# Second round of the feed-forward set into the first, two batches' sums to one PSUM bank, and changed ends of the attention in a block of feed-forward, attention and feed-forward

## The chip, the cores and the metric

One Trainium2 chip, one core of it. The metric is the device time of one execution in microseconds (us). TensorE is called PE here, VectorE DVE, ScalarE ACT, GpSimd POOL, and SyncE SP; SP only issues DMAs. A DMA that POOL issues has its descriptors written by POOL itself.

## What is computed

The input x is 8 batches of 2048 tokens of 256 floats. A token-routed feed-forward is applied with half weight, then an attention, then the same feed-forward again. All arithmetic is fp32 (the attention's scores and values run through fp32r tiles in part).

```python
x = x + 0.5 * ffn(layernorm(x))        # ffn returns its input, with 128 rows a batch replaced
x = x + attn(layernorm(x))
x = x + 0.5 * ffn(layernorm(x))

def ffn(x):                            # x: (8, 2048, 256)
    _, idx = top_k(x @ w_router, 128)              # 128 tokens of each batch, in order of score
    x_sel = take(x, idx)
    h = rmsnorm(x_sel, g1)
    q, k, v = split(h @ W_qkv.T)                   # 16 heads of 16
    att = softmax(causal(q @ k.T / 4))             # 128 x 128 a head
    x_attn = (att @ v) @ W_out.T
    h2 = rmsnorm(x_sel + x_attn, g2)
    x_ff = silu(h2 @ W1.T) * (h2 @ W2.T) @ W3.T    # 682 wide
    return x.at[idx].set(x_sel + x_attn + x_ff)

def attn(x):                           # 8 heads of 32, all 2048 tokens of a batch
    q, k, v = (lowrank(x, U, V) + b for each)
    return softmax(q @ k.T / sqrt(32)) @ v
```

## The kernel before

The program is a row of blocks; between two of them all engines meet at a barrier and the block's semaphores are cleared. `score_rows` reads all rows, takes their statistics and router scores. `pick_tokens` finds the 128 best of each batch and keeps their row numbers in `picked`. `routed_ffn` gathers those rows, computes the feed-forward on them and scatters them back. `project` makes keys, queries and values of all tokens. `attend` is the attention. Then `score_rows`, `pick_tokens` and `routed_ffn` once more, now on the sum of `after_ffn` and `attention`. Each engine has its own list of instructions, written by hand in the order in which it takes them, and waits on semaphores. An engine that waits holds up all that stands behind in its list.

**Reading.** In the second `score_rows` SP loads pieces of 4 tiles (128 rows each) of both addends, 512 KB each. The addend goes into a ring of `NADD = 6` buffers; a load waits until the sum of six pieces earlier is done (`added`). POOL adds each piece (L198) and makes one product (L191).

**Picking.** Each batch is cut in four lists. DVE finds the 128 best of every list, then for each batch b counts for each candidate how many are better (L474), turns the rank into a 0/1 table `is_rank` (L484), and PE multiplies this table by the row numbers (L516), which gives the rows in order in `prow`. After the last batch one DVE copy (L489) turns all of `prow` into `picked`, and the block ends. ACT scales all other rows beside this and stores them.

**Feed-forward.** Two rounds (`ROUNDS`) of `NB = 4` batches. POOL first issues all gathers: 8 in the first feed-forward (L649), 16 in the second (L649 and L652), then makes constants, and in the second adds the two gathered parts (L672). One round is, in this order on PE: turn the normalised rows (L910), keys and queries (L917), values (L926), for each batch the scores of all 16 heads into banks 0 to 3 (L937), for each batch turn the probabilities and multiply by the values (L949, L961), output projection (L967), turn the second norm's rows (L973), six `up` steps (L984, two projections of 128 columns each) and six `down` steps (L993) that sum into banks 0 to 3, a bank for each batch. DVE spreads the keys by head (L757), adds the causal mask (L764), takes the row maximum (L768), normalises six of sixteen heads (L775; POOL does ten, L681), combines the values' halves (L789), and gates (L810, L812). ACT does the exponentials, 16 a batch (L869), copies out of PSUM and the tanh of the gate (L896). Round 1 begins when round 0's `down` has been issued.

**Attention.** 64 units (batch, four heads, 512 queries). A unit's scores come in 64 tiles; ACT takes the exponential (L1703). Before that the row maximum is found one unit ahead: PE writes 4 score tiles into `ps_max` (L1736), DVE reduces three of them (L1592), ACT copies the fourth (L1655) and DVE reduces the copy (L1594); 16 such fours a unit. For unit 0 this stands alone at the start, with one set of four banks: PE writes the next four only when both readers are done. Its loads are `load_q(0, 0)` and `load_kv(0, 0)` on SP, all of them landed before PE starts. The sum of a unit's probabilities is made by POOL (L1562) on nine of sixteen chunks and by accumulating DMAs that POOL issues (L1541, seven pairs of chunks, `DMA_PAIRS`); PE sums over partitions (`close_z`, L1792), then two sets of turns and a DVE multiplication end the unit.

## Time and profile before

| | us |
|---|---|
| median of 3 runs | 4295.17 (4293.64 to 4295.38) |
| profiled execution | 4294.03 |
| its span, first to last instruction | 4292.0 |
| 0 to 171 | first reading and picking |
| 171 to 434 | first feed-forward |
| 434 to 721 | projections |
| 721 to 796 | attention: loads, row maxima of unit 0 |
| 796 to 3791 | attention: 64 units |
| 3791 to 3816 | attention: end of the last unit |
| 3816 to 4012 | second reading and picking |
| 4012 to 4292 | second feed-forward |

Over the span PE is busy 84%, DVE 74%, ACT 76%, POOL 70%. The rows of the section further down are of this one execution; times in them count from the span's start.

### The profile page before, as it was taken

To read this page: it belongs to the slowest core of one execution; us is meant where nothing else is said; L and a number is where in the kernel's file an instruction comes from. 1 tells how busy PE (TensorE), PEld (TensorE's weight loads), DVE (VectorE), ACT (ScalarE), POOL (GpSimd) and SP (SyncE) were. 2 spreads that over 40 slices of the span, in tenths; PEclk is the share of its full clock that TensorE was granted. 3 is DMA by queue.
4 is the path that set the end of the run, shared out by engine and by line. 5 is a ranking of instruction groups with operands and counts; after the bars stand their busy time and mean duration, and the time that the engine had idled before them with its cause. 6 is when DMAs were issued, how large, how long until landed. Compare 5 with 4: busy or idle time off the path is not lost. (4 is left out here: it accounts for less than half of the span.)

```text
span 4292.0 us, 59690 instructions
## 1 busy us (share of the span) xinstructions
PE 3592.8 (84%) x20178; PEld 1422.3 (33%) x20178; DVE 3187.8 (74%) x4122; ACT 3242.9 (76%) x6717; POOL 2988.4 (70%) x1166
## 2 busy tenths in 40 slices
PE   0376784699999999999999999999999999930376
PEld 0243452233333333333333333333333333310243
DVE  8644674888888888888888888888888888628544
ACT  3544673589988898998898899899889989834433
POOL 2011001399999999999999999999999989975211
PEclk9988897799999999999999999999999999965598
DMA  6500899589999999999999999999999999888300
GB/s 210 168 5 3 296 391 313 118 180 194 210 198 204 206 199 205 198 212 198 204 207 197 207 196 209 202 202 208 198 207 200 206 202 195 170 214 277 124 5 5
DMA packets 335683, 809.46 MB, mean 189 GB/s; under 512 B 27596, under 2 KB 211424, under 8 KB 271648
## 3 DMA queue, kind: packets, MB, share of 16 engines
q0 software_dynamic: 66432, 475.04, 54.9%
q1 hardware_dynamic: 223008, 284.46, 22.7%
q10 hardware_dynamic: 45952, 46.27, 3.1%
q8 instruction: 159, 2.61, 0.2%
q14 instruction: 132, 1.08, 0.1%
HBM read 198.90 MB, written 136.48 MB: 78 GB/s over the span
## 5 line engine op out<-in xcount | busy, mean ns | idle before, releaser
L1703 ACT ACTIVATE at_probs<-at_ps_s 128x512 f32<-128x512 f32 x4096 | 2261.9, 615 | 256.4 <-PE at_ps_s L1813 248.9
L1562 POOL TENSOR_TENSOR at_pool_sum<-at_pool_sum,at_probs 128x2048 f32<-128x2048 f32 x448 | 2173.6, 4852 | 27.8 <-DMA at_probs<-at_probs 20.0
L1592 DVE TENSOR_REDUCE at_part_max<-at_ps_max 128x3 f32<-128x1536 f32 x1024 | 1801.0, 1759 | 428.6 <-PE at_ps_max L1736 428.3
L1813 PE MATMUL at_ps_s<-at_qs,at_ks 97*128 97x512 f32 (+1 forms) x4096 | 1524.4, 451 | 6.4 <-ACT at_probs L1703 5.1
L1782 PE MATMUL at_ps_acc<-at_probs,at_v 128*32 128x512 f32 x8192 | 1092.7, 605 | 0.9 <-ACT at_probs L1703 0.9
L1813 PEld LDWEIGHTS at_ps_s<-at_qs,at_ks 97*128 97x128 f32 (+1 forms) x4096 | 626.5, 188 | 1103.5 <-ACT at_probs L1703 815.5
L1594 DVE TENSOR_REDUCE at_part_max<-at_max_copy 128x1 f32<-128x512 f32 x1024 | 691.7, 675 | 0.0
L1655 ACT COPY at_max_copy<-at_ps_max 128x512 f32<-128x512 f32 x1024 | 610.0, 596 | 102.2 <-PE at_ps_max L1736 102.0
L1541 POOL DMA_DIRECT2D at_probs<-at_probs x448 | 399.7, 892 | 288.4 <-ACT at_probs L1703 240.1
L1736 PE MATMUL at_ps_max<-at_ks,at_qs 32*128 32x512 f32 x4096 | 525.5, 500 | 83.0 <-DMA at_ks<-qk_parts 49.3
L1736 PEld LDWEIGHTS at_ps_max<-at_ks,at_qs 32*128 32x128 f32 x4096 | 197.8, 183 | 442.2 <-issue 393.4
L1562 POOL TENSOR_TENSOR at_pool_sum<-at_probs 128x2048 f32<-128x2048 f32 x64 | 313.0, 4891 | 0.1
L1782 PEld LDWEIGHTS at_ps_acc<-at_probs,at_v 128*32 128x32 f32 x8192 | 161.2, 108 | 346.3 <-ACT at_probs L1703 299.4
L1525 POOL MEMSET at_ones<- 128x128 f32 x1 | 0.2, 204 | 285.9 <-POOLq L62 285.9
L681 POOL TENSOR_TENSOR f_att<-f_att,f_rowsum 128x1280 f32<-128x1280 f32 x16 | 49.5, 3097 | 182.3 <-DVE f_rowsum L773 182.3
L285 PE MATMUL s_pt<-s_ident,s_small 128*128 128x128 f32 x2 | 0.9, 448 | 203.6 <-DVE s_small L254 203.6
L75 ACT ACTIVATE rows_tile<-rows_tile,rows_affine 128x256 f32<-128x256 f32 x256 | 129.3, 587 | 19.1 <-ACT rows_tile L75 13.8
L1607 DVE RECIPROCAL at_rz<-at_ps_s 128x16 f32<-128x16 f32 x64 | 16.5, 257 | 169.6 <-PE at_ps_s L1799 169.6
L1255 PE MATMUL pr_pqk<-pr_xT,pr_w 128*128 128x512 f32 x256 | 124.0, 629 | 16.2 <-ACT pr_xT L1202 12.0
L869 ACT ACTIVATE f_att<-f_att,f_rowmax 128x128 f32<-128x128 f32 x256 | 98.7, 388 | 47.7 <-DVE f_rowmax L769 47.7
L1155 DVE SCALAR_TENSOR_TENSOR pr_lo<-pr_pqk,lr_bias,pr_hi 128x512 fp32r<-128x512 f32 x128 | 88.4, 744 | 40.4 <-ACT pr_hi L1214 37.1
L224 DVE BATCH_NORM_STATS2 s_stats<-rows_tile 128x6 f32<-128x256 f32 x256 | 101.2, 419 | 20.2 <-POOL rows_tile L198 20.2
(196 smaller groups left out, 2405.0 us busy)
## 6 DMA issues: line engine op xcount, KB each, us to landing
at_probs<-at_probs POOLq DMA_DIRECT2D x448, 1024.0 KB, 8.3
qk_parts<-pr_hi SPq DMA_DIRECT2D x32, 1024.0 KB, 12.1
qk_parts<-pr_lo SPq DMA_DIRECT2D x32, 1024.0 KB, 12.3
at_qs<-qk_parts SPq DMA_DIRECT2D x320, 64.0 KB, 5.5
at_ks<-qk_parts SPq DMA_DIRECT2D x80, 256.0 KB, 5.2
rows_tile<-in_x SPq DMA_DIRECT2D x16, 1024.0 KB, 11.9
after_ffn<-rows_tile ACTq DMA_DIRECT2D x16, 1024.0 KB
v_tokens<-pr_v SPq DMA_DIRECT2D x32, 512.0 KB, 10.9
```

The costliest lines, as they stand in the source:

```text
L75: return nc.scalar.activation(self.tile[:, b, t, :], self.tile[:, b, t, :], ACT.Identity, scale=self.affine[:, 0, b, t:t + 1], bias=self.a ...
L224: nc.vector.bn_stats(stats[:, b, t, :], rows.tile[:, b, t, :]).then_inc(stats_done, 1)
L1255: nc.tensor.matmul(pqk[:, m, :], w[:, m // NG, m % NG, :], xT[:, n % 2, m % NG, :], start=True, stop=True).then_inc(qk_done, 1)
L1541: nc.gpsimd.dma_start(probs[:, slot(unit, a)], probs[:, slot(unit, c)], accum_op=ALU.add).then_inc(dma_added[(unit * ND + d) % MERGES_OUT] ...
L1562: nc.gpsimd.tensor_tensor(acc, first, probs[:, slot(unit, c)], ALU.add).then_inc(pool_added, 1)
L1592: nc.vector.reduce_max(part_max[:, 0:HG - 1, t, c], ps_max[:, 0:HG - 1], AX.X).then_inc(three_max_done, 1)
L1594: nc.vector.reduce_max(part_max[:, HG - 1:HG, t, c], max_copy[:, n % 2:n % 2 + 1], AX.X).then_inc(part_max_done, 1)
L1655: nc.scalar.copy(max_copy[:, n % 2], ps_max[:, HG - 1]).then_inc(max_copied, 1)
L1703: nc.scalar.activation(probs[:, slot(unit, c), h], ps_s[:, BANK[unit, j]], ACT.Exp, scale=SCALE).then_inc(exp_done, 1)
L1736: last = nc.tensor.matmul(ps_max[:, h], qs[rows, unit % NQB, h, t * P:(t + 1) * P], ks[rows, un % BU // NU, h, c * 512:(c + 1) * 512], sta ...
L1782: last = nc.tensor.matmul(ps_acc[h * DH:(h + 1) * DH, :], v[:, k // NU, c, h * DH:(h + 1) * DH], probs[:, slot(n, c), h], start=(c == 0), ...
L1813: nc.tensor.matmul(ps_s[:, BANK[unit, j]], ks[rows, g, h, c * P:(c + 1) * P], qs[rows, unit % NQB, h, :], start=True, stop=True).then_inc( ...
```

## The change

Six things are edited.

1. **Feed-forward order.** `qT` and `v` get a buffer for each round. Keys, queries, values of round 1 are issued between the score steps of round 0. A batch's scores are now two half steps of 8 heads in two banks (`bank_scores`), masked one half at a time. Round 1's scores, masks and exponentials are issued between the `up` and `down` steps of round 0. After them comes round 1 from the turned probabilities on, as before. POOL does all eight multiplications, then all eight scatters.
2. **`down` banks.** Two batches' sums share a bank (banks 0 and 1); the last row step waits for both of a bank.
3. **Gathers.** A new class `Gathered` holds `xs`, `ads` and their semaphores; POOL issues batch b's gathers inside `pick_tokens` as soon as `picked` has that batch. `is_rank` has two buffers instead of one for each batch, and the copy into `picked` is made batch by batch.
4. **Buffers.** To make room, `NADD` goes from 6 to 4 and the scrap buffers of `score_rows` from 4 to 2.
5. **Attention start.** Only the high parts of unit 0's queries (SP) and keys (ACT's queue) are loaded first, and PE waits for those alone; SP issues the rest once they have landed. Unit 0's maxima use two sets of four banks in turn (`first_banks`).
6. **Attention end.** The last unit has five POOL additions instead of eight and six accumulating DMAs instead of seven; `close_z_of_last` lets PE sum five sources (two raw chunks, two DMA sums, the POOL sum) instead of one.

```diff
 def pick_tokens
+            for b in range(B):
+                pool.wait_ge(picked_done, b + 1)
+                gathered.gather(b)
...
+                if b >= 1:
+                    copy_picked(b - 1)
-                nc.vector.tensor_tensor(is_rank[:, first:end, :],
+                nc.vector.tensor_tensor(is_rank[:, b % 2],
...
-            dve.wait_ge(ordered, 1)
-            nc.vector.tensor_copy(picked, prow[:]).then_inc(picked_done, 1)
-            dve.wait_ge(picked_done, 1)
+            copy_picked(B - 1)
 def routed_ffn, tensor
+            def scores(i, k):
+                s, g = k // 2, k % 2
+                if k == 0:
+                    pe.wait_ge(qT_copied, i * NC + NC)
+                    pe.wait_ge(v_copied, i + 1)
+                pe.wait_ge(spread_done, at(i, s))
+                if i == 0 and k >= 2:
+                    pe.wait_ge(masked_done, k - 1)
+                elif i > 0:
+                    pe.wait_ge(masked_done, i * HALVES + k)
...
+            up(0, 0)
+            scores(1, 0)
+            up(0, 1)
+            up(0, 2)
+            scores(1, 1)
+            put_down(0, 0)
+            up(0, 3)
+            scores(1, 2)
...
+            scores(1, 7)
+            put_down(0, 5)
+            turn_probs_and_pv(1)
 routed_ffn, vector
+            mask(1, 0)
+            gate(0, 0)
+            mask(1, 1)
+            gate(0, 1)
+            mask(1, 2)
+            gate(0, 2)
+            mask(1, 3)
+            normalize(1, 0)
+            gate(0, 3)
+            mask(1, 4)
+            mask(1, 5)
+            normalize(1, 1)
+            gate(0, 4)
+            mask(1, 6)
+            gate(0, 5)
+            mask(1, 7)
 attend, sync
-            load_q(0, 0)
-            load_kv(0, 0)
+            for to, first, end in HI_ROWS:
+                sp.dma_start(qs[to:to + DH, 0, first:end].bitcast(F32), src[0, 0, :, first:end, 0:UQ]).then_inc(hi_in, 16)
+            sp.wait_ge(hi_in, 2 * len(HI_ROWS) * 16)
...
 attend, tensor
-            pe.wait_ge(q_in[0], LOADS)
-            pe.wait_ge(k_in[0], LOADS)
+            pe.wait_ge(hi_in, 2 * len(HI_ROWS) * 16)
...
+                        sources = [probs[:, slot(n, c)] for c in LAST_RAW]
+                        for d in LAST_PAIRS:
+                            m = n * ND + d
+                            pe.wait_ge(dma_added[m % MERGES_OUT], (m // MERGES_OUT + 1) * 16)
+                            sources.append(probs[:, slot(n, DMA_PAIRS[d][0])])
+                        pe.wait_ge(pool_added, n * ADDS + LAST_ADDS)
+                        sources.append(pool_sum[:, k % 2])
```

PE at the start of a feed-forward, before (L910 turns rows, L917 keys and queries, L926 values, L937 scores, L949 turns probabilities):

```order
L910 MATMUL f_ps<-f_ident,f_hn 128x128 x8
L917 MATMUL f_ps<-f_hT,w_wqkv 128x512 x8
L926 MATMUL f_ps<-w_wqkv,f_hT 128x256 x8
L937 MATMUL f_ps<-f_kspread,f_qT 128x512 x16
L949 MATMUL f_ps<-f_ident,f_att 128x128 x16
```

The same place in the changed kernel (L1007, L1015, L1035, L1050, L1065 are the same five steps):

```order
L1007 MATMUL f_ps<-f_ident,f_hn 128x128 x8
L1015 MATMUL f_ps<-f_hT,w_wqkv 128x512 x8
L1035 MATMUL f_ps<-w_wqkv,f_hT 128x256 x8
L1050 MATMUL f_ps<-f_kspread,f_qT 128x512 x4
L1007 MATMUL f_ps<-f_ident,f_hn 128x128 x8
L1050 MATMUL f_ps<-f_kspread,f_qT 128x512 x4
L1015 MATMUL f_ps<-f_hT,w_wqkv 128x512 x4
L1050 MATMUL f_ps<-f_kspread,f_qT 128x512 x4
L1015 MATMUL f_ps<-f_hT,w_wqkv 128x512 x4
L1050 MATMUL f_ps<-f_kspread,f_qT 128x512 x4
L1035 MATMUL f_ps<-w_wqkv,f_hT 128x256 x8
L1065 MATMUL f_ps<-f_ident,f_att 128x128 x16
```

Round 1's turns, keys, queries and values have moved in front of round 0's turned probabilities.

ACT after the second norm of round 0, in the changed kernel (L953 the last copy of the norm, L961 tanh, L930 exponentials of round 1, L941 the copies of turned probabilities); before, all six tanh (L896) stood in a row there:

```order
L953 ACTIVATE f_hT<-f_ps,w_gain 128x512 x2
L961 ACT_TABLE_LOAD
L961 ACTIVATE f_sig<-f_ps 128x512 x2
L930 ACTIVATE f_att,f_rowsum<-f_att,f_rowmax 128x128 x16
L961 ACTIVATE f_sig<-f_ps 128x512 x2
L930 ACTIVATE f_att,f_rowsum<-f_att,f_rowmax 128x128 x16
L961 ACTIVATE f_sig<-f_ps 128x512
L961 ACTIVATE f_sig<-f_ps 42x512
L930 ACTIVATE f_att,f_rowsum<-f_att,f_rowmax 128x128 x32
L941 COPY f_attT<-f_ps 128x1024 x8
```

The four exponential groups of round 1 now stand among and behind round 0's tanh steps.

POOL around the end of picking, before (L440 the last constant of the picking block, L368 and L644 its end and the next block's start):

```order
L440 CAST t_floats<-t_ints 128x192
L368 UNCONDITIONAL_BRANCH
L61 ISA
L644 UNCONDITIONAL_BRANCH
L649 DMA f_xs<-in_x,picked 128x256 x8
L655 MEMSET f_ones 128x128
```

And now:

```order
L462 CAST t_floats<-t_ints 128x192
L372 DMA g_xs<-in_x,picked 128x256 x8
L390 UNCONDITIONAL_BRANCH
L61 ISA
L678 UNCONDITIONAL_BRANCH
L681 MEMSET f_ones 128x128
```

The gathers have moved from behind the block boundary to ahead of it.

## Rows read from the trace of the kernel before

**Rows 1.** Busy time in stretches: us, each engine's busy us (instructions), PE clock, DMA share, GB/s
```profile
796.00:3746.00 2950.00, 2942.48 (x17173) 1038.59 (x17169) 2430.84 (x2198) 2644.05 (x5227) 2692.60 (x942) 1.00 0.95 199
...
4047.00:4166.00 119.00, 87.48 (x384) 48.66 (x384) 52.49 (x83) 51.89 (x170) 12.39 (x4) 0.86 0.00 1
```

**Rows 2.** Order of time (start, us, instruction, idle before), end of second picking, DVE and PE
```profile
4006.23 0.60 DVE L474 TENSOR_SCALAR_CACHE_REDUCE t_junk<-t_all_top,t_topT 128x384 f32<-128x384 f32 x1
...
4009.89 1.87 PE L516 MATMUL t_prow<-t_rowT,t_is_rank 128*128 128x1 f32 x8 [1.65 <-DVE t_is_rank L484]
...
4011.80 0.17 DVE L489 CAST picked<-t_prow 128x8 uint32<-128x8 f32 x1 [1.96 <-PE t_prow L516]
```

**Rows 3.** The chain that ended last (start, us, what), gathers of the second feed-forward
```profile
4013.73 1.09 POOL f_xs L649
...
4032.68 0.94 POOL f_ads L652
...
4035.13 2.74 POOL f_xs L672 x4
```

**Rows 4.** First feed-forward in order of time: POOL's first gather, DVE's first step behind the constants
```profile
171.45 1.16 POOL L649 DMA_INDIRECT f_xs<-in_x,picked  x1 [80.39 <-POOLq L62]
...
182.91 0.16 DVE L703 TENSOR_REDUCE f_parity<-f_head_of 128x2 f32<-128x8 f32 x1 [10.55 <-POOL f_head_of L666]
```

**Rows 5.** Attention start in order of time: PE's first four, then DVE
```profile
743.47 0.80 PE L1736 MATMUL at_ps_max<-at_ks,at_qs 32*128 32x512 f32 x4 [49.28 <-DMA at_ks<-qk_parts]
...
746.98 1.76 DVE L1592 TENSOR_REDUCE at_part_max<-at_ps_max 128x3 f32<-128x1536 f32 x1 [0.32 <-PE at_ps_max L1736]
```

**Rows 6.** DMA issues from 720 to 800: size each, median us to landing
```profile
at_ks<-qk_parts SPq DMA_DIRECT2D x10, 256.0 KB, 6.8
```

**Rows 7.** Attention end in order of time: PE a unit earlier and at the end, POOL
```profile
3762.22 1.04 PE L1792 MATMUL at_ps_s<-at_pool_sum,at_ones 128*32 128x512 f32 x8
...
3806.85 1.94 PE L1792 MATMUL at_ps_s<-at_pool_sum,at_ones 128*32 128x512 f32 x8 [15.52 <-POOL at_pool_sum L1562]
...
3785.88 1.61 POOL L1541 DMA_DIRECT2D at_probs<-at_probs  x1
...
3792.22 14.48 POOL L1562 TENSOR_TENSOR at_pool_sum<-at_pool_sum,at_probs 128x2048 f32<-128x2048 f32 x3
```

**Rows 8.** DMA issues from 3740 to 3816, and from 3816 to 3936: size, median us to landing
```profile
at_probs<-at_probs POOLq DMA_DIRECT2D x9, 1024.0 KB, 7.6
...
s_addend<-attention SPq DMA_DIRECT2D x32, 512.0 KB, 8.9
```

**Rows 9.** POOL's last two additions of the second reading
```profile
3915.24 2.35 POOL L198 TENSOR_TENSOR rows_tile<-rows_tile,s_addend 128x1024 f32<-128x1024 f32 x1
...
3918.23 2.35 POOL L198 TENSOR_TENSOR rows_tile<-rows_tile,s_addend 128x1024 f32<-128x1024 f32 x1
```

**Rows 10.** The chain that ended last, second feed-forward
```profile
4046.99 1.95 PE f_ps L910 x8
...
4131.72 13.38 PE f_ps L984 x24
...
4146.83 3.43 PE f_ps L984 x8
...
4205.42 12.42 ACT f_att L869 x64
```

**Rows 11.** Groups by line from 4047 to 4284: count, busy us, mean ns of one
```profile
L764 DVE TENSOR_TENSOR f_att<-f_ps,f_causal 128x2048 f32<-128x2048 f32 x8 | 18.3, 2288 | 10.1 <-PE f_ps L937 10.1
L768 DVE TENSOR_REDUCE f_rowmax<-f_att 128x16 f32<-128x2048 f32 x8 | 18.3, 2286 | 0.3
...
L810 DVE SCALAR_TENSOR_TENSOR f_act<-f_sig,f_ps 128x512 f32<-128x512 f32 (+1 forms) x12 | 8.2, 686 | 52.5 <-ACT f_sig L896 52.5
L775 DVE TENSOR_TENSOR f_att<-f_att,f_rowsum 128x768 f32<-128x768 f32 x8 | 7.7, 958 | 0.3
L896 ACT ACTIVATE f_sig<-f_ps 128x512 f32<-128x512 f32 (+1 forms) x12 | 7.2, 596 | 49.7 <-PE f_ps L984 49.7
```

More of the change, by code:

```diff
@@ new lines, in final_row @@
+            def final_row(i, s):
+                dve.wait_ge(down_done, at(i, s | 1))
+                own.step(nc.vector.tensor_tensor(proc[:, s, :], down(s), xr[:, s, :], ALU.add))
+                if i > 0:
+                    dve.wait_ge(row_out, i * NB * 16)
+                nc.vector.scalar_tensor_tensor(row[:, s, :], proc[:, s, :], 0.5, xs[:, at(i, s) - 1, :],
+                                               ALU.mult, ALU.add).then_inc(row_done, 1)
+            for s in range(NB):
+                spread(0, s)
@@ new lines, in _ @@
+            mask(1, 0)
[14 more added lines that the diff above has]
+            mask(1, 7)
+            normalize(1, 2)
+            for s in range(NB):
+                final_row(0, s)
+            normalize(1, 3)
@@ L830, in _ @@
+            for s in range(NB):
+                even_and_odd(1, s)
+            second_norm(1)
+            for f in range(DFF_TILES):
+                gate(1, f)
+            for s in range(NB):
+                final_row(1, s)
         @block.scalar
@@ L920, in _ @@
-                last.then_inc(qk_done, 1)
-                if i > 0:
-                    pe.wait_ge(row_done, i * NB)
+                for g in range(NC):
+                    for c in range(NC):
+                        last = nc.tensor.matmul(ps[:, bank + g, :], wqkv[:, c, which * D + g * P:which * D + (g + 1) * P],
+                                                hT[:, c].rearrange("p s t -> p (s t)"), start=(c == 0),
+                                                stop=(c == NC - 1))
+                last.then_inc(done, 1)
@@ new lines, in put_down @@
+            def put_down(i, f):
+                m = rows_of(f)
+                pe.wait_ge(gated_done, i * DFF_TILES + f + 1)
+                for s in range(NB):
+                    last = nc.tensor.matmul(down(s), gatedT[0:m, f, s, :], w3[0:m, f, :],
+                                            start=(f == 0 and s % 2 == 0),
+                                            stop=(f == DFF_TILES - 1 and s % 2 == 1))
+                    if f == DFF_TILES - 1:
+                        last.then_inc(down_done, 1)
@@ new lines, in _ @@
+            turn_rows(0)
+            keys(0)
+            queries(0)
+            values(0)
+            scores(0, 0)
+            scores(0, 1)
+            turn_rows(1)
+            scores(0, 2)
+            scores(0, 3)
+            keys(1)
+            scores(0, 4)
+            scores(0, 5)
+            queries(1)
+            scores(0, 6)
+            scores(0, 7)
+            values(1)
+            turn_probs_and_pv(0)
+            second_norm(0)
+            pe.wait_ge(spread_done, 2 * NB)
```

513 lines of the change are left out of this document (305 added, 208 removed).

## The prediction

> **What bounds the kernel now.** I read the busy time by stretches first, then the chain that ended last, then each end of the attention in order of time. [rows 1] split the kernel in two. In the 2950 us of the attention's units PE is busy 2942 us and all else follows; the change leaves that stretch alone. In a round of the second feed-forward (119 us) PE is busy 87.5 us, DVE 52 and ACT 52: no engine is full, so a chain of hand-overs sets the time, and what counts is which step follows which. The other places that the change touches are waits too: in [rows 3] the second feed-forward starts with POOL's 16 gathers; in [rows 5] PE waits for the keys; in [rows 7] PE stands 15.52 us for POOL's sum. The sum is made for the profiled 4294.03 us, 1.1 us below the median; I add that at the end.
>
> **Gathers.** The copy into picked ends at 4011.97 [rows 2], the first gather starts 1.76 us later, the last ends at 4033.62, constants take 1.5 us, and the first addition starts at 4035.13 [rows 3]. A batch is ranked every 3.52 us (PE's 1.87 busy and 1.65 idle [rows 2]), and its two gathers cost 2.5 us (16 from 4013.73 to 4033.62 [rows 3]), so now 14 of 16 lie beside the ranking. DVE makes seven more copies of 0.17 us with some 0.03 us between: 1.4 us on the path. New start: 4011.97 + 1.4 + 2.5 + 1.76 + 1.5 = 4019.1, a gain of 16.0 us. In the first feed-forward there is one gather a batch: of 11.46 us between the first gather and DVE's first step [rows 4] seven gathers of 1.25 us go, less 1.4: 7.4 us. Together **23.4 us**. Bounds: 26.2 (copies hidden) and 0 (every gather waits until the ranking is over). I take a value near the upper one, since in [rows 2] DVE counts 384 elements in 0.60 us with a new instruction every half microsecond: nothing there is long.
>
> The Trainium skill speaks against this place. By SBUF — State Buffer, section "SBUF: two separate sides", DVE in a two-port mode locks POOL out of the port through which it writes DMA descriptors, and a DMA of about 620 ns then takes about 3100 ns. By that figure 16 gathers would take about 50 us beside 28 us of ranking, an estimate that puts the start of the second feed-forward about where it was. No row here shows a gather beside DVE's work.
>
> **Attention start.** PE starts at 743.47 [rows 5], when all sixteen transfers of unit 0 are in. The block starts at 720.9. Now eight transfers go first, four of 64 KB on SP and four of 256 KB on ACT's queue, issued side by side at about 0.5 us each, the last at 722.8; a piece of 256 KB lands in 6.8 us [rows 6], which gives 729.6; I take 729.0, because less is queued: 14.5 us. Bounds: 8 (landing twice as slow) and 16.5 (DVE's own clearing of the tiles ends at 727). Then the sixteen fours of unit 0: DVE idles 0.32 us before each [rows 5], because PE may write the next four only when both readers are done. With two sets of banks PE writes ahead: 15 x 0.32 = 4.8 us; bounds 0 and 4.8. What is late next is DVE itself, 2.35 us a four. The rest of the loads now starts behind the wait, 8 us into the block; all of them ended 47 us after the block's start before, so they should end near 771, while unit 0's first scores are due near 777. They are covered with about 6 us to spare. **19.3 us.**
>
> **Attention end.** POOL's last three additions run from 3792.22 for 14.48 us; PE's sum starts at 3806.85 and takes 1.94 [rows 7]. Now the last transfer that is waited for is the one issued at 3785.88 [rows 7]; it lands 7.6 us later [rows 8], near 3794. POOL's fifth addition ends at 3792. PE then does five groups instead of one: 1.04 us each at the full clock or 1.94 at the low one [rows 7], so 5.2 or 9.7. PE has paused 3 us and not 15.5, so I take a mix, 7.0: 3801. The turns behind it gain 0.7 us at the faster clock. 3808.8 - 3801 + 0.7 = **8.5 us**; bounds 4 and 11.
>
> **Feed-forward.** The largest edit. I work on the second feed-forward in three pieces and double the result.
> Front, first turn (4046.99) to first up step (4131.72): 84.7 us [rows 10]. PE now also does round 1's turns (1.0 us), keys and queries (6.9) and values (3.4) in it. They stand between score steps, where DVE and PE hand over, and ACT's four exponential groups (6.2 us each, two in 12.42 [rows 10]) cover most. Cost between 0 and 11.3 us; I take 2.5, because one keys piece and the mask behind it delay one group by that much and the rest lies under the exponentials.
> Middle, first up step to the end of round 1's exponentials: 4131.72 to 4217.84 (4205.42 + 12.42), 86.1 us [rows 10]. The new chain, with an up step 3.43 [rows 10], half a score step or a down step 1.72 (half of it), half a mask 1.15, maximum and scaling 2.46, normalising with its reciprocal 1.2, tanh 0.6, gate 1.4 [rows 11], exponentials 6.2:
> - three up steps and two half scores 13.7; half a mask and the maximum 3.6; exponentials of batch 0 6.2, and tanh 2 stands behind them on ACT; tanh 2 and gate 2 2.0: 25.5
> - up step 4 and half 3 5.2; mask, maximum, normalising, gate 3 6.2: 36.9
> - up step 5, halves 4 and 5 with a mask each (one pair of banks, so each half waits for the mask before) 9.2; maximum, normalising, gate 4 5.1: 51.2
> - down 4 and half 7 3.4; mask and maximum 3.6; exponentials of batch 3 6.2: 64.4
> Some 25 hand-overs of 0.15 to 0.2 us make 4 to 5. PE's low clock after pauses costs about 3 us where it falls worst: 24 products of the up steps take 13.38 where 10.3 is full speed [rows 10]. I take 4 to 5 for that too: 73.5, a gain of 12.5. Bounds: 21 (no low clock, hand-overs free) and 0 (the chain interleaved one for one).
> Tail, from round 1's turned probabilities on: as before, but the last row step waits for a pair of batches, 0.4 us, and the first probabilities are turned early: even.
> 12.5 - 2.5 = 10 us a feed-forward, **20 us** for both. The ACT order in the section on the change loads no table between tanh and exponentials, so switching is free. POOL's scatters of round 0 now wait behind its multiplications of round 1; only round 1's row steps wait for them, 60 us later.
>
> **Reading.** Between POOL's additions pass 2.99 us [rows 9]. With four buffers the load of a piece may start 3 x 2.99 + 0.7 = 9.7 us ahead of its use. Its second half is issued 1.4 us in and lands 8.9 us later [rows 8], with six pieces queued: 10.3. Were the landing to stay so, a loop over four buffers would be 0.6 us longer, 0.15 us a piece, 5 us over 32. But a queue of four pieces is shorter than one of six. I take 0; bounds 0 and 5. The scrap buffers cost nothing: each waits for the sum two back, which had ended before the last one began.
> By the Trainium skill, DMA: Bandwidth & Descriptors, section "Anatomy of one DMA", a transfer costs about 2.0 us plus its bytes at 436 GB/s. By that, 512 KB alone are an estimated 3.2 us, and the cost would be nil as well.
> One more semaphore clearing behind each feed-forward: the whole block change with one of them is 1.76 us, so less than that each; **1 us** for both.
>
> **Sum.** 23.4 + 19.3 + 8.5 + 20 - 1 = 70.2. 4294.03 - 70.2 = 4223.8; to the median, 4225.
>
> **Rivals.** (a) The new feed-forward order gains nothing: tanh steps queued behind exponentials and masks behind gates take all back. For it: every list is now one chain through both rounds; against: the steps above sum to 64 and not 86. 4225 + 20 = 4245. (b) The gathers get through only when the ranking is over: 4225 + 23.4 = 4248. (c) The reading waits for buffers: 4230. (d) Slower than before, by PE's clock. A round has PE busy 87.5 us at a granted clock of 0.86 of 2.4 GHz [rows 1]: 75 us at the full clock, 150 at 1.2 GHz. If the many pauses of 3 to 8 us in the merged stretch kept it at 1.2 GHz throughout, a feed-forward would last 300 us and some 20 of pauses, against 237: 4225 + 20 + 2 x 83 = 4411. It outweighs the other gains (50 us) once a feed-forward is 25 us longer than before, at a mean clock of about 0.7. Against it: the scores of round 0 already alternate with pauses of 2 to 3 us, and the round still has 0.86.
>
> **How the numbers follow.** Forecast 4225, chance 0.74; by the likelier parts of its bounds it lies between 4207 and 4242. (a) 0.12, (b) 0.05, (c) 0.06, (d) 0.02, anything else 0.01. From 4204 to 4248 lie (a), (b), (c) and all of the forecast but its far tails: the range. 0.2% (9 us) is about what a measurement of this kernel can tell from no change. All but (d) and half of the remainder are faster by more: faster 0.97, same 0.01, slower 0.02.
>
> **What the profile after would show.** The first addition of the second feed-forward 7 us behind the last pick, with 14 gathers ended before it; PE's first product of the attention 8 us into its block and fours 2.35 us apart; the first score 19 us earlier; PE's last sum starting 3 us after its last values product; a middle stretch of 70 to 77 us in both feed-forwards; POOL's additions of the second reading still 3.0 us apart. I am wrong if gathers stretch far past 1.3 us beside DVE, if PE's clock in the merged stretch falls under 0.8, or if the 64 units between change.

## The result, and the profile after

The changed kernel takes 4232.93 us (median of 4 runs, 4230.27 to 4234.5) against 4294.53 us before (4 runs, 4293.64 to 4295.38): ratio 0.9855, 95% interval 0.9842 to 0.9869. That is 61.6 us less; 70 were forecast. The profiled execution has a span of 4232.8 us (4292.0 before), and its parts can be laid beside the terms of the forecast:

| term | forecast | in the two traces |
|---|---|---|
| gathers | 23.4 | 22.2 (7.0 and 15.2) |
| attention start | 19.3 | 19.9 |
| attention end | 8.5 | 9.7 |
| feed-forward, both | 20 | 11.8 |
| reading of the second scores | 0 | 0 (0.3 lost, counted in the gathers' 15.2) |
| hand-over around the feed-forwards | -1 | 0.2 (0.8 lost behind the first, 1.0 won behind the second) |
| the 64 units | 0 | -4.5 |
| sum | 70.2 | 59.2 (4292.0 - 4232.8; the rows above add to 0.1 more by rounding) |

In the views below, rows between those shown are left out.

**Gathers.** POOL and DVE in order of time at the end of the ranking, second feed-forward (start us, duration us, engine, line; in brackets the idle time before it and what ended it):

```profile
3973.31 0.68 DVE L515 TENSOR_TENSOR t_is_rank<-t_floats,t_rank 128x512 f32<-128x512 f32 x1
3973.66 1.15 POOL L372 DMA_INDIRECT g_xs<-after_ffn,picked  x1 [1.19 <-DVE picked L491]
3975.11 0.94 POOL L375 DMA_INDIRECT g_ads<-attention,picked  x1 [0.30 <-issue]
3975.95 0.16 DVE L491 CAST picked<-t_prow 128x1 uint32<-128x1 f32 x1 [1.96 <-PE t_prow L545]
3976.38 0.94 POOL L372 DMA_INDIRECT g_xs<-after_ffn,picked  x1 [0.32 <-DVE picked L491]
3977.63 0.94 POOL L375 DMA_INDIRECT g_ads<-attention,picked  x1 [0.30 <-issue]
3983.26 5.48 POOL L698 TENSOR_TENSOR g_xs<-g_xs,g_ads 128x256 f32<-128x256 f32 x8
```

From the last pick to the first addition 7.3 us pass where [rows 2, 3] have 23.3. POOL waits 1.18 to 1.19 us for each pick but the last: it has time to spare. The table's 15.2 is counted from the attention's result (222.9 us from there to the first addition before, 207.7 now). So it holds what is lost on the way there, 0.8 us: 0.3 in the reading, and 0.4 in the ranking, where a batch takes 3.58 us instead of 3.52.

The first gather of a pair takes 1.15 us and the second 0.94 or 0.95, as long as gathers took before with DVE idle (0.94 to 0.98, the first of all 1.09). In the pairs ahead of this one the second lies beside DVE's counting, so the counting costs it nothing; the first lies beside the step that makes `is_rank` (L515, 0.68 us). A pause of POOL is not the reason: the last gather of the first feed-forward stands behind a pause of 1.57 us, with DVE idle, and takes 0.94. The 3100 ns of the Trainium skill, SBUF — State Buffer, section "SBUF: two separate sides", are not what this trace shows; that figure is given beside a `tensor_copy` of DVE, and DVE's only copies near a gather here take 0.16 us and read PSUM, so the case in which it was measured did not arise.

**Attention start.** SP's and ACT's queues start their block at 709.35, DVE at 710.26. PE and DVE in order of time from there:

```profile
718.16 0.80 PE L1944 MATMUL at_ps_max<-at_ks,at_qs 32*128 32x512 f32 x4 [34.91 <-DMA at_ks<-qk_parts]
719.01 1.76 DVE L1790 TENSOR_REDUCE at_part_max<-at_ps_max 128x3 f32<-128x1536 f32 x1 [3.67 <-PE at_ps_max L1944]
721.28 1.75 DVE L1790 TENSOR_REDUCE at_part_max<-at_ps_s 128x3 f32<-128x1536 f32 x1
723.53 1.75 DVE L1790 TENSOR_REDUCE at_part_max<-at_ps_max 128x3 f32<-128x1536 f32 x1
```

PE starts 8.8 us into its block (22.6 before, [rows 5]); DVE no longer idles between fours, which are 2.26 us apart. The first score of the units comes 55.4 us into the block instead of 75.3.

**Attention end.** PE and DVE at the end:

```profile
3763.34 1.07 PE L1993 MATMUL at_ps_acc<-at_probs,at_v 128*32 128x512 f32 x8 [0.94 <-ACT at_probs L1906]
3766.89 5.34 PE L2019 MATMUL at_ps_s<-at_probs,at_ones 128*32 128x512 f32 x32 [2.49 <-DMA at_probs<-at_probs]
3772.02 1.07 PE L2019 MATMUL at_ps_s<-at_pool_sum,at_ones 128*32 128x512 f32 x8
3775.54 0.69 DVE L1821 TENSOR_TENSOR at_o<-at_ps_s,at_rz 128x512 f32<-128x512 f32 x1 [0.81 <-PE at_ps_s L2033]
```

The wait is 2.49 us where [rows 7] have 15.52, and it is now one for a transfer. From the last values product to the result: 12.2 us instead of 21.9.

**Feed-forward.** Cut as in the prediction (front: first turn to first up step; middle: to the end of round 1's exponentials; tail: to the last row step), in us, first and second feed-forward:

| kernel | front | middle | tail |
|---|---|---|---|
| before | 83.6, 84.7 | 85.8, 86.1 | 66.2, 66.4 |
| changed | 88.6, 88.0 | 75.4, 75.9 | 66.3, 67.0 |

The front lost 4.9 and 3.3, the middle won 10.4 and 10.2. PE and then ACT in order of time in the front of the second feed-forward:

```profile
4017.18 3.60 PE L1050 MATMUL f_ps<-f_kspread,f_qT 128*128 128x512 f32 x8
4027.84 5.25 PE L1015 MATMUL f_ps<-f_hT,w_wqkv 128*128 128x512 f32 x8 [7.07 <-ACT f_hT L914]
4032.93 3.60 PE L1050 MATMUL f_ps<-f_kspread,f_qT 128*128 128x512 f32 x8
...
4026.47 1.23 ACT L914 ACTIVATE f_hT<-f_ps,w_gain 128x512 f32<-128x512 f32 x2
4040.36 0.40 ACT L930 ACTIVATE f_att<-f_att,f_rowmax 128x128 f32<-128x128 f32 x1 [6.50 <-DVE f_rowmax L792]
```

PE has turned round 1's rows by 4017.3, and ACT, but for a table load, is idle until 4020.29; but the copy (L914) stands behind the exponentials of batch 0, so PE waits 7.07 us for it with the scores of batch 2 queued behind, and ACT then waits 6.50 us for these. The middle, PE's up steps, eight instructions each:

```profile
4083.16 6.62 PE L1105 MATMUL f_ps<-f_hT,w_w 128*128 128x512 f32 x8 [1.36 <-ACT f_hT L953]
4091.33 7.03 PE L1105 MATMUL f_ps<-f_hT,w_w 128*128 128x512 f32 x16
4105.23 5.40 PE L1105 MATMUL f_ps<-f_hT,w_w 128*128 128x512 f32 x8 [3.43 <-DVE f_gatedT L830]
4114.98 3.70 PE L1105 MATMUL f_ps<-f_hT,w_w 128*128 128x512 f32 x8 [0.90 <-DVE f_gatedT L830]
4126.71 5.25 PE L1105 MATMUL f_ps<-f_hT,w_w 128*42 128x512 f32 x8 [4.59 <-DVE f_gatedT L830]
```

At full speed a step is 3.60 in this view and two are 7.03. The steps behind pauses of 3.43 and 4.59 us, and the one behind the second norm's pauses (3.17 us, the turns, 1.36 us), take 1.7 to 3.0 us more. By stretches (front, middle, tail; us, busy time of PE, its weight loads, DVE, ACT and POOL with counts, granted clock, DMA share, GB/s):

```profile
3995.20:4083.20 88.00, 62.56 (x329) 36.68 (x329) 52.93 (x80) 50.00 (x169) 12.39 (x4) 0.89 0.00 1
4083.20:4159.00 75.80, 55.50 (x136) 27.03 (x136) 35.27 (x42) 29.56 (x136) 9.29 (x3) 0.86 0.00 0
4159.00:4226.00 67.00, 54.09 (x304) 32.33 (x304) 20.86 (x48) 17.34 (x24) 8.84 (x7) 0.91 0.03 11
```

### The profile page after: what moved, and what is told of

Its sections match the earlier page's. It is cut to its first block and busy times, and to the rows that moved or that the text cites. A ratio compares the mean times of both kernels' runs of the same rounds, so it can differ in the third digit from the quotient of the medians.

```text
span 4232.8 us, 59845 instructions
## 1 busy us (share of the span) xinstructions
PE 3595.9 (85%) x20210; PEld 1426.4 (34%) x20210; DVE 3191.8 (75%) x4152; ACT 3241.4 (77%) x6717; POOL 2976.3 (70%) x1162
## 3 DMA queue, kind: packets, MB, share of 16 engines
q14 instruction: 133, 1.09, 0.1%
## 5 line engine op out<-in xcount | busy, mean ns | idle before, releaser
L930 ACT ACTIVATE f_att<-f_att,f_rowmax 128x128 f32<-128x128 f32 x256 | 98.8, 389 | 97.0 <-DVE f_rowmax L792 97.0
L1105 PE MATMUL f_ps<-f_hT,w_w 128*128 128x512 f32 (+1 forms) x192 | 102.6, 690 | 23.3 <-DVE f_gatedT L830 17.9
L786 DVE TENSOR_TENSOR f_att<-f_ps,f_causal 128x1024 f32<-128x1024 f32 x32 | 39.0, 1223 | 106.3 <-PE f_ps L1050 106.3
```

Source lines behind the costliest of these rows:

```text
L930: last = nc.scalar.activation(att[:, s, h], att[:, s, h], ACT.Exp, scale=ATT_SCALE, bias=rowmax[:, s, h:h + 1], accum_out=rowsum[:, s, h:h ...
L1105: last = nc.tensor.matmul(ps[0:m, bank_up(f, which), :], w[:, c, f * P:f * P + m], hT[:, c].rearrange("p s t -> p (s t)"), start=(c == 0), ...
```

## The experiments

Two theories for the 8 us missing in the feed-forward: **places in queues** (ACT's copy behind exponentials, gates behind row maxima) and **PE's clock** (1.2 instead of 2.4 GHz after pauses). Each run is compared with the changed kernel, 4232.93, which was measured with the result only. The kernel before was measured again beside the runs: 4295.09, 4294.34 and, beside the last three (late gathers, three and two buffers), 4291.77, against 4294.53 with the result. So two medians of one kernel differ by up to 3.3 us, and the intervals of the ratios are some 6 us to each side; what is smaller than that is read from positions in the traces.

### One copy ahead on ACT

```diff
+            turned_rows(1)
             exponentials(0, 0)
-            turned_rows(1)
             exponentials(0, 1)
```

> The changed kernel with one step moved on ACT: the copy of round 1's turned rows (hT) now stands ahead of the exponentials of batch 0, in both feed-forwards. In the trace of the changed kernel PE waits 7.07 us for that copy before round 1's keys, and the exponentials of batch 2 start 6.50 us late. Theory A (the front of a feed-forward lost its 3 to 5 us by this place in ACT's queue): the wait of 7 us goes, PE computes the keys at once, exponentials of batch 2 follow those of batch 1 with under 1 us between, the front shrinks by 6 to 7 us in each feed-forward: 12 to 14 us faster than the changed kernel, near 4220. Rival B (the front lost it by PE doing round 1's products between the scores, and DVE's masks behind normalising): the wait only moves to the masks, 0 to 3 us faster in all, 4230 to 4233.

Measured: 4219.59 us (5 runs, 4218.26 to 4224.11), 13.3 less; ratio to before 0.9828 (0.9815 to 0.9841). PE, then ACT, in order of time:

```profile
4008.17 3.60 PE L1050 MATMUL f_ps<-f_kspread,f_qT 128*128 128x512 f32 x8
4011.60 3.60 PE L1015 MATMUL f_ps<-f_hT,w_wqkv 128*128 128x512 f32 x8
...
4008.37 1.26 ACT L914 ACTIVATE f_hT<-f_ps,w_gain 128x512 f32<-128x512 f32 x2 [4.68 <-PE f_ps L1007]
4011.28 0.40 ACT L930 ACTIVATE f_att<-f_att,f_rowmax 128x128 f32<-128x128 f32 x1 [0.35 <-DVE f_rowmax L792]
```

The copy fills an idle time of ACT and PE's wait is gone. The fronts are 80.2 and 80.7 us: 8.3 and 7.3 less than in the changed kernel, 3.4 and 4.0 less than before the change (the tails are 1.9 and 1.4 longer). Theory A holds: what the prediction called a cost of PE's extra work was one place in one list.

### Gates ahead of row maxima

The middle in another order. DVE's list (ACT: tanh 2 and 3 ahead of the exponentials of batch 0, tanh 4 ahead of those of batch 1; PE: down step 3 between score steps 4 and 5, 4 between 5 and 6, 5 between 6 and 7):

```diff
             mask(1, 0)
             gate(0, 0)
-            mask(1, 1)
+            mask(1, 1, False)
             gate(0, 1)
-            mask(1, 2)
             gate(0, 2)
+            row_max(1, 0)
+            mask(1, 2)
+            gate(0, 3)
             mask(1, 3)
             normalize(1, 0)
-            gate(0, 3)
             mask(1, 4)
+            gate(0, 4)
             mask(1, 5)
             normalize(1, 1)
-            gate(0, 4)
-            mask(1, 6)
             gate(0, 5)
+            mask(1, 6)
             mask(1, 7)
             normalize(1, 2)
```

> The changed kernel with another order in the middle stretch of both feed-forwards (same instructions): on DVE the gates of steps 1 and 2 stand ahead of the row maximum of batch 0, and the others ahead of masks; on ACT tanh 2 and 3 stand ahead of the exponentials of batch 0, which wait 8.3 us there anyway; on PE each late down step stands between two score steps, and the last score step ahead of nothing but the turns. In the changed kernel PE waits 3.43, 0.90, 4.59, 1.41 and 2.87 us there for DVE (13.2 us) and the up steps take 28.0 us of 20.6 at full speed. Theory D (places in ACT's and DVE's queues bound the middle): PE's waits halve or better, and fewer pauses bring up steps back to speed: 8 to 14 us a feed-forward, 16 to 28 us faster than the changed kernel, 4205 to 4217. Rival (PE's clock bounds it, whatever the order, or the exponentials of the last batch end no earlier): 0 to 6 us faster in all.

Measured: 4215.82 us (5 runs, 4212.67 to 4218.92), 17.1 less; ratio 0.9815 (0.9801 to 0.9828). The middles are 64.7 and 64.8 us, 10.6 and 11.1 less; one front and one tail are some 2 us longer. PE, then ACT's last exponentials:

```profile
4097.12 3.70 PE L1109 MATMUL f_ps<-f_hT,w_w 128*128 128x512 f32 x8 [0.91 <-DVE f_gatedT L833]
4104.10 3.60 PE L1109 MATMUL f_ps<-f_hT,w_w 128*128 128x512 f32 x8
4126.35 3.65 PE L1118 MATMUL f_ps<-w_w,f_gatedT 42*128 42x256 f32 x8 [2.85 <-DVE f_gatedT L833]
...
4137.42 0.40 ACT L934 ACTIVATE f_att<-f_att,f_rowmax 128x128 f32<-128x128 f32 x1 [7.28 <-DVE f_rowmax L795]
```

The steps that had stood behind pauses of 3.43 and 4.59 us run at full speed, now that one stands behind 0.91 us and the other behind none: order and clock gain together. What is late now is the last score step, queued behind a down step that waits 2.85 us for the last gate.

### Both orders

As the two runs above, and three more places. On PE the last score step stands ahead of the last down step. On DVE the last mask but one (`mask(1, 6)`) stands ahead of the last gate, and the normalising of batch 1 behind the last mask; the last mask itself stays behind the last gate. PE's part:

```diff
             put_down(0, 4)
             scores(1, 6)
-            put_down(0, 5)
             scores(1, 7)
+            put_down(0, 5)
```

> The changed kernel with both new orders: the copy of round 1's turned rows ahead of the exponentials of batch 0 (13.3 us by itself), and the gates-ahead middle (17.1 by itself) with one more move: the last score step and its mask stand ahead of the last down step and the last gate, since in that run PE stood 2.85 us for the last gate with the last scores behind it and the last exponentials began 7.28 us late. Theory D (queue places set the time, and the two stretches do not touch each other): 13 + 17 and 5 to 7 more in each feed-forward, 40 to 44 us faster than the changed kernel, 4189 to 4193. Rival (the late move only shifts the wait to the last gate, as the exponentials of batch 2 delay those of batch 3): 30 us, 4203.

Measured: 4181.97 us (5 runs, 4176.42 to 4185.48), 51.0 less than the changed kernel; ratio 0.9739 (0.9726 to 0.9752). Fronts 80.5 and 81.0, middles 58.1 and 58.2, tails 66.3: the sum of these against the changed kernel is 51. The late moves together are worth 6.6 us a feed-forward in the middles (58.1 for 64.7): the last exponentials start 0.75 us after ACT is free. Which of the three does it was not taken apart. The gain is above the 40 to 44 that were expected: 13.3, 17.1 and twice 6.6 are 43.6, and of the rest most is that the tails and the one front that were some 2 us longer in each of the two single runs are not longer here. The two stretches do add, and none takes from the other.

```profile
4095.33 0.40 ACT L934 ACTIVATE f_att<-f_att,f_rowmax 128x128 f32<-128x128 f32 x1 [0.75 <-DVE f_rowmax L795]
```

### Pauses filled with products

Products of no use in the second norm, behind the output projection and behind the turns (the two waits ahead of the fillers stood ahead of the first up step):

```diff
                     last.then_inc(proj_done, 1)
+                if i == 0:
+                    pe.wait_ge(spread_done, 2 * NB)
+                    pe.wait_ge(v_copied, 2)
+                for _ in range(7):
+                    nc.tensor.matmul(ps[:, bank_up(0, 0), :], ident[:], wqkv[:, 0, 0:512], start=True, stop=True)
...
                 last.then_inc(h2_turned, 1)
+                for _ in range(3):
+                    nc.tensor.matmul(ps[:, bank_up(0, 0), :], ident[:], wqkv[:, 0, 0:512], start=True, stop=True)
                 pe.wait_ge(h2T_done, i * NC + NC)
```

> The changed kernel with products of no use put into two pauses of PE in every second norm: seven 128x512 products behind the output projection, three behind the turns, into a bank that the first up step overwrites. Nothing is left out. In the changed kernel the turns there take 1.65 us and the first eight products of the up step 6.6 (second feed-forward, round 0), and 24 take 13.5 in round 1, where 10.3 is full speed. Theory C (what the middle stretch missed of its forecast, and a like loss in round 1, is PE at the low clock after these pauses): with the pauses filled the first up step takes 3.4 to 3.6 us, the turns 1.1; 3.2 + 0.6 us come back four times, less some overshoot: 10 to 15 us faster than the changed kernel, 4218 to 4223. Rival: the clock does not stay up for products of no use, or the pauses are not what lowers it: no gain, and 0 to 4 us slower where the fillers run over.

Measured: 4232.28 us (4 runs, 4230.16 to 4233.61), no difference from the changed kernel. By the time alone the rival holds; by the trace it does not:

```profile
4073.48 6.17 PE L1095 MATMUL f_ps<-w_wqkv,f_ident 128*128 128x512 f32 x14
4082.94 3.60 PE L1112 MATMUL f_ps<-f_hT,w_w 128*128 128x512 f32 x8
```

The first up step is at full speed (3.60 for 6.62). But each filler is two instructions and 0.86 us, twice what I had counted, so that seven of them (6.0 us) outlast the pause of 3.17 us by 3: fronts 92.5 and 92.3 (3.9 and 4.3 more), middles 70.8 and 72.5 (4.5 and 3.4 less), tails 69.0 and 68.1 (2.8 and 1.1 more). The overrun took the gain and 4 us more, which in this trace shorter units (2991.9 us, see below) cover. Hence the same with 3 and 1:

> The changed kernel with the fillers of the earlier run cut to what the pauses hold: a 128x512 product took 0.86 us there (seven took 6.0 in a pause of 3.17, three 2.6 in one of 1.36, and so ran 2.9 and 1.2 us over, four times in all), so now three stand behind the output projection and one behind the turns. Nothing is left out. Theory C (the low clock behind these pauses costs 3 us and more at each of four places; the earlier run showed the first up step at 3.60 instead of 6.62, and gave it back by running over): the clock stays up and nothing runs over, 3 to 4 us at each of four places, 10 to 15 us faster than the changed kernel, 4218 to 4223. Rival (the short fill leaves pauses of 0.5 us twice, and the clock still falls): 0 to 3 us faster.

Measured: 4217.23 us (5 runs, 4213.8 to 4224.96), 15.7 less; ratio 0.9823 (0.981 to 0.9837).

```profile
4065.89 2.74 PE L1095 MATMUL f_ps<-w_wqkv,f_ident 128*128 128x512 f32 x6
4069.23 1.64 PE L1099 MATMUL f_ps<-f_ident,f_hn 128*128 128x128 f32 x8 [0.60 <-ACT f_hn L949]
4070.70 1.02 PE L1103 MATMUL f_ps<-w_wqkv,f_ident 128*128 128x512 f32 x2
4072.22 3.70 PE L1112 MATMUL f_ps<-f_hT,w_w 128*128 128x512 f32 x8 [0.49 <-ACT f_hT L953]
```

Pauses of 0.5 to 0.6 us are left and the up steps keep their speed. Middles 72.7 and 72.6 (2.7 and 3.3 less), tails 64.0 (2.3 and 3.0 less), fronts 0.4 less: 12 us of the 15.7 have a place. The clock's price is shown, and it is in the kernel before as well: [rows 10] have 13.38 for 24 instructions. It is not one number: behind the same pause of 1.35 or 1.36 us the first up step of round 0 takes 5.1 to 5.3 us in nine feed-forwards and 6.2 to 6.7 in eleven, over the ten traces without fillers; in all six feed-forwards with fillers it takes 3.60 or 3.70.

### Orders, fillers and the attention's end

The kernel of both orders, the fillers (3 and 1) in the second norms, three behind the first variance and one behind the first turns, and at the attention's end the sources that are in ahead of the wait for the last transfer:

```diff
-                        for d in LAST_PAIRS:
+                        for d in LAST_PAIRS[:-1]:
...
                         for at, (source, ready, value) in enumerate(sources):
+                            if ready is not None:
+                                pe.wait_ge(ready, value)
```

> The kernel of orders_only with fillers: three and one in each second norm as in fill_fitted, three behind the first variance and one behind the first turns ahead of the keys (which take 9.73 us where 6.9 is full speed), and at the attention's end the products of the sources that are in already ahead of the wait for the last transfer (PE stands 2.49 us there and then takes 6.2 for five groups). Theory C: 12 us by the second norms, 3 in front of each feed-forward's keys, 3 at the attention's end: about 20 us below orders_only, 4170 to 4176. Rival (with tighter orders there are no pauses long enough to lower the clock, so only the ends gain): 5 us below orders_only.

Measured: 4160.89 us (5 runs, 4159.28 to 4161.76), 72.0 less than the changed kernel and 133 less than before; ratio to before 0.9688 (0.9675 to 0.9701). This is the fastest version here, below both kernels. Stretches of the second feed-forward (columns as above), and PE at the attention's end:

```profile
3954.70:4032.40 77.70, 62.97 (x338) 36.78 (x339) 52.79 (x81) 50.25 (x169) 12.39 (x4) 0.96 0.00 1
4032.40:4089.10 56.70, 47.01 (x136) 24.08 (x136) 34.45 (x36) 29.69 (x136) 9.18 (x3) 0.95 0.00 1
4089.10:4153.00 63.90, 54.48 (x312) 32.65 (x312) 23.34 (x55) 17.28 (x23) 8.86 (x8) 0.95 0.03 11
```

```profile
3726.89 1.07 PE L2008 MATMUL at_ps_acc<-at_probs,at_v 128*32 128x512 f32 x8 [0.94 <-ACT at_probs L1921]
3727.77 2.76 PE L2038 MATMUL at_ps_s<-at_probs,at_ones 128*32 128x512 f32 x24
3731.35 1.06 PE L2038 MATMUL at_ps_s<-at_probs,at_ones 128*32 128x512 f32 x8
```

The granted clock is 0.95 to 0.96 where it was 0.86 to 0.91. Most of that in the middle is the orders' work: with both orders alone it is 0.88, 0.94 and 0.90, with the short fillers alone 0.90, 0.89 and 0.95. Against both orders alone the fronts are shorter by 3.1 and 3.3 us, the middles by 1.4 and 1.5, the tails by 1.4 and 2.4, the attention's end by 4.2 (8.0 instead of 12.2, and PE has no pause left in its sums). The whole step took 21.1 us off, as expected (about 20), but not by the expected parts: middles and tails, where the fillers of the second norms act, give 6.7 of 12, the fronts 6.4 of 6, the end 4.2 of 3, and the rest has no place in the traces.

### Parts undone

The feed-forward before put back, all else kept:

> The changed kernel with the feed-forward before put back (its lists, its banks, down steps a batch to a bank), early gathers and all else kept. By the two traces the new order is worth 5.5 us in the first feed-forward and 6.3 in the second (front 4.9 and 3.3 lost, middle 10.4 and 10.2 won). Theory A (the term of 20 us was oversized, the others right): 11 to 13 us slower than the changed kernel, 4244 to 4246. Rival (the term was right and something else is lost elsewhere): about 20 us slower, 4253.

Measured: 4243.98 us (4 runs, 4239.72 to 4244.7), 11.1 more. The term was 20; it is 11 to 12, by the time and by the positions.

The attention before put back, all else kept:

> The changed kernel with the attention before put back, start and end, all else kept. By the two traces the start is worth 19.9 us (block start to first score) and the end 9.7 (last values product to the last result), and the 64 units took 4.5 us more in the one profiled run of the changed kernel, 3.6 of it in one unit in which POOL waited 2.6 us for a late transfer. Theory A (that loss is chance): 29 to 30 us slower than the changed kernel, 4262. Rival (the units do lose 4.5 us by the new ends): 25 us slower, 4258.

Measured: 4264.3 us (5 runs, 4261.05 to 4268.33), 31.4 more. It has before's attention, and its 64 units took 2997.0 us where before's took 2994.0. In the eleven traces with the new ends (the changed kernel and the ten other runs) they took 2991.9 to 3000.1, on average 2996.8. So the -4.5 us of the table lie inside a scatter of 8 us; a mean loss of 2 us is not excluded by so few traces.

The gathers moved back behind the ranking:

```diff
-            for b in range(B):
-                pool.wait_ge(picked_done, b + 1)
-                gathered.gather(b)
```

> The changed kernel with the gathers moved back behind the ranking, to the start of the feed-forward's own part of POOL's list; picks still copied one by one. By the two traces early gathers are worth 7.0 us in the first feed-forward (gathers to DVE's first step) and 15.2 in the second. Theory A (gathers beside DVE's ranking cost no more than alone): 22 to 24 us slower than the changed kernel, 4255 to 4257. Rival (part of the 22 is the reading or the weights' loading): 15 us slower, 4248.

Measured: 4260.34 us (5 runs, 4256.52 to 4262.48), 27.4 more, above both expectations. In its trace the last pick is 23.1 us ahead of the first addition (7.3 in the changed kernel: 15.8 more), and the first feed-forward's first turn comes 7.3 us later: 23.1 in all. Of the other 4.3, 1.6 are that the changed kernel's traced run stands that much above its median, and 1.3 lie behind the last row step; the rest is spread over the trace. The three parts undone sum to 69.9 against 61.6 for the whole; by positions in the traces they are 63.6.

Fewer buffers in the second reading (four in the changed kernel, six before):

```diff
-    NADD = 4
+    NADD = 3
```

> The changed kernel with three buffers for the second reading's addend where it has four. POOL's additions stand 3.0 us apart in both kernels, with four and with six buffers. Theory A (the transfers' time from issue to landing is mostly waiting in the queue, so that it shrinks with the queue, and the stream of 349 GB/s sets the pace): no change, within 3 us of the changed kernel. Rival (the landing of 8.9 us stays, as the prediction's rule for the cost had it): the load of a piece starts 2 x 2.99 + 0.7 = 6.7 us ahead of its use and is in 10.3 us after it, 3.6 us late every three pieces, 1.2 us a piece, 38 us over 32: 4271.

> The changed kernel with two buffers for the second reading's addend. Theory A (queue wait): a load starts 3.7 us ahead of its use; the stream itself needs 3.0 us a piece of 1 MB, so a part of the fixed time of a transfer (1.6 to 2.5 us for 64 to 256 KB alone, in the traces) shows: 1 to 1.5 us every piece, 30 to 50 us slower than the changed kernel, 4265 to 4280. Rival (landing of 8.9 us whatever the queue): 10.3 - 3.7 = 6.6 us every two pieces, 3.3 a piece, 106 us slower, 4339.

Measured: 4236.34 us with three (4 runs, 4231.04 to 4237.24; 3.4 more) and 4260.41 with two (5 runs, 4256.18 to 4264.28; 27.5 more). POOL's additions by line (count, busy us, mean ns, idle before them), with four, three and two, and the issues of the addend (size, median us to landing) with four, three and two:

```profile
L199 POOL TENSOR_TENSOR rows_tile<-rows_tile,s_addend 128x1024 f32<-128x1024 f32 x32 | 75.1, 2345 | 8.5 <-DMA s_addend<-attention 8.5
```

```profile
L199 POOL TENSOR_TENSOR rows_tile<-rows_tile,s_addend 128x1024 f32<-128x1024 f32 x32 | 75.3, 2352 | 9.2 <-DMA s_addend<-attention 8.6 <-ACT s_act_junk L271 0.6
```

```profile
L199 POOL TENSOR_TENSOR rows_tile<-rows_tile,s_addend 128x1024 f32<-128x1024 f32 x32 | 74.9, 2342 | 36.6 <-DMA s_addend<-attention 36.4
```

```profile
s_addend<-attention SPq DMA_DIRECT2D x32, 512.0 KB, 8.9
```

```profile
s_addend<-attention SPq DMA_DIRECT2D x32, 512.0 KB, 6.1
```

```profile
s_addend<-attention SPq DMA_DIRECT2D x32, 512.0 KB, 5.1
```

The landing is mostly queue: it shrinks from 8.9 to 6.1 with one buffer less, and the additions stay 3.0 us apart. From the attention's result to the last addition pass 106.1 us with six buffers, 106.4 with four, 106.5 with three and 134.5 with two, so three cost nothing that a trace shows, although the median is 0.4 us past the 3 us allowed for. With two the landing is 5.1 where a load may start only 3.7 us ahead of its use, and the pace falls to 3.9 us a piece. Theory A holds twice; its estimate for two buffers (30 to 50) was a little high. From six to four, however, the landing did not shrink: it is 8.9 in [rows 8] too. In both kernels SP takes 1.42 us to issue most of these loads, with three and two buffers 0.51; a queue that is full in both would look like this, but that is argued and not shown.

## Why the prediction was right, and where not

**Right.** Sign, size and the place in the range, because three of the four terms were waits that end at one known event, and the event that came next could be read from a row: the pick ahead of the last pair of gathers, the first eight transfers, the last transfer of a pair. They came out at 22.2, 19.9 and 9.7 for 23.4, 19.3 and 8.5. Two of these sums agree better than their parts. In the gathers of the second feed-forward the copies cost 0.4 us and not 1.4, but from POOL's last gather to its first constant pass 3.24 us and not 1.76. At the attention's start PE begins 13.8 us earlier for 14.5, and the fours give 6.1, above the bound of 4.8, since they are 2.26 us apart and not 2.35. That these misses nearly cancel is luck. At the attention's start the loads that were put behind the wait did not become late. At its end the pause was 2.49 us for 3 forecast and the five groups took 6.2 for 7.0. Rival (b) is refuted by POOL's waits for the picks, (c) by the additions' unchanged 3.0 us. Rival (d) needed a mean clock of 0.7; it is 0.86 to 0.91.

**Right, but not for the reason given.** The reading was put at 0 because a queue of four pieces would be shorter than one of six. The landing stayed at 8.9 us. By the prediction's rule that should have cost 5 us, and the traces have 0.3: the rule counts a landing that is mostly queue as time that a load needs. The estimate of 3.2 us for 512 KB was met by no load here either; the fastest of them took 3.8.

**Wrong: the feed-forward, 11.8 for 20.** Two steps of it:

- The front's cost, 2.5, "because one keys piece and the mask behind it delay one group by that much": it was 4.9 and 3.3, and the reason given was not the one at work. I walked PE's and DVE's lists and took ACT's four groups of exponentials as cover, but did not ask where in ACT's own list the copy stands that PE's keys wait for. It stands behind 6.2 us of exponentials; moving it gave 13.3 us.
- The middle, 73.5 for 75.4 and 75.9. The chain of hand-overs was right in its order and nearly in its length; the clock was not. "4 to 5" was taken for PE's low clock, and by the rows above up steps alone took 6.6 us more than at full speed (in the second feed-forward). The fillers showed that 3 of them hang on the second norm's two pauses, and gates_ahead that the others hang on waits for gates.

Rival (a) said that tanh behind exponentials and masks ahead of gates would take all back. They took part of the 8 us that are missing of the 20: 4.4 are missing in the middles, where such places and the clock act together, 3.2 in the fronts, by ACT's copy, and 0.7 in the tails. Of what there was to gain, places in lists took far more: with both orders put right the feed-forward edit is worth 63 us (11.8 and 51.0). I priced the lists as given and never asked what they could have been.

**Not settled:** why the first gather of a pair is 0.2 us longer beside DVE's `is_rank` step, what decides between 5.2 and 6.6 us for the up step behind the same pause, and whether the units lose up to 2 us on average.

## What to carry to other kernels

When a second round is set into a first one, walk every engine's list, also that of the engine that seems only to cover: a short copy that another engine waits for goes ahead of a long group as soon as its input exists, and what feeds the matrix engine goes ahead of what only feeds a reduction. Then look at the duration of the first products behind each pause: where they are slow, first remove the pause by order, and fill with products of no use only what is left, a little shorter than the pause; behind a better order they are worth less (6.7 us in middles and tails here, where they gave 11.3 before it). Before counting on a cover, or on a filler, take its length from a row of the same shape.

## What the runs showed of the hardware

**Products of no use hold PE's clock.** Behind pauses of 3.17 and 1.36 us the first up step took 5.1 to 6.7 us, in 20 feed-forwards; with 2.74 and 1.02 us of such products in these pauses it took 3.70, in four. The granted clock of the second feed-forward's tail rose from 0.91 to 0.95 by them, and that of the middle from 0.86 to 0.89; the orders alone raised the middle's to 0.94.

**DVE held up by POOL.** In both feed-forwards of the changed kernel a row step of DVE falls beside POOL's multiplication. DVE, then POOL:

```profile
4153.81 0.42 DVE L836 TENSOR_TENSOR f_proc<-f_ps,f_xr 128x256 f32<-128x256 f32 x1
4154.26 2.10 DVE L840 SCALAR_TENSOR_TENSOR f_row<-f_proc,g_xs 128x256 f32<-128x256 f32 x1
...
4152.98 3.10 POOL L704 TENSOR_TENSOR f_att<-f_att,f_rowsum 128x1280 f32<-128x1280 f32 x1 [8.61 <-DVE f_rowsum L796]
```

L840 took 2.10 us instead of 0.43 and ended 0.3 us behind POOL's instruction; L836, with one operand in PSUM, was not held. By the Trainium skill, SBUF — State Buffer, section "SBUF: two separate sides", a DVE instruction with two inputs in SBUF and a POOL instruction that reads SBUF exclude each other from a shared pair of ports for the whole instruction; the rows agree. It cost nothing here, since nobody waited for this row step. The kernel before has it as well, in steps of four columns beside POOL's additions of 0.73 us (L672), three in a row that take 0.65 us instead of 0.17:

```profile
4038.59 0.65 DVE L731 TENSOR_TENSOR f_small<-f_stats 128x4 f32<-128x4 f32 x1
```

**A landing time is not a property of the transfer.** The same 512 KB landed in 8.9, 6.1 and 5.1 us with four, three and two buffers. Between four and three the stream of data kept its pace, so the difference is time in the queue, and a bound computed with the landing of the longer queue is too high.
